# Routed experts of a four-layer transformer: routing weights spread over the rows by DMA from DRAM in place of a picking matmul

## The reference

```python
scores = softmax(xf @ Wg)                        # [4096, 32]
weights, indices = top_k(scores, 4)              # 4 experts for each token
for e in range(32):
    # the first 2048 tokens that chose e, with their weight w
    out = (silu(xg @ W1[e]) * (xg @ W3[e])) @ W2[e] * w[:, None]
    y = y.at[tok].add(out)
z = (silu(xf @ Ws1) * (xf @ Ws3)) @ Ws2
x = x + attention(xn) + y + z
```

## Time and profile before

| | us |
|---|---|
| median of 3 runs | 3521.24 (3521.11 to 3521.61) |
| the profiled execution, its own time | 3524.08 |
| its span in the profile | 3522.1 |
| TensorE busy over the span | 3236.2 (92%) |
| mean granted TensorE clock over the span | 0.96 of full |

### The profile page before, as it was taken

The page is one execution under the profiler, slowest core; times in us unless marked ns, Lnnn a source line. Parts: engine busy times, 40 slices in busy tenths (PEclk is TensorE's granted clock), DMA queues, the critical chain, the costliest instruction groups (busy, mean ns, idle before and its releaser), DMA issues.

```text
span 3522.1 us, 73076 instructions
## 1 busy us (share of the span) xinstructions
PE 3236.2 (92%) x24822; PEld 2369.4 (67%) x24823; DVE 2505.3 (71%) x5419; ACT 2384.3 (68%) x7079; POOL 1901.2 (54%) x1809
## 2 busy tenths in 40 slices
PE   5999969998769996999997999999999999999997
PEld 3777646665558885757665677766777677676775
DVE  6888768883676666444345778887788777877776
ACT  4777748885335555624523888888888888888885
POOL 4222132221235553401203888888888888888884
PEclk9999969999779997999997999999999999999998
DMA  3222132220000003000000000000000000000000
GB/s 104 71 70 73 40 122 73 76 70 1 1 1 1 1 1 103 13 1 1 1 1 13 2 2 2 2 1 2 1 2 1 2 2 2 1 2 2 2 2 25
DMA packets 54894, 78.25 MB, mean 22 GB/s; under 512 B 5952, under 2 KB 43648, under 8 KB 54272
## 3 DMA queue, kind: packets, MB, share of 16 engines
q1 hardware_dynamic: 54528, 73.58, 6.5%
HBM read 54.69 MB, written 18.87 MB: 21 GB/s over the span
## 4 chain that ended last, share of the span: by engine, by line
PE 45%; POOL 6%; ACT 4%; DVE 3%; issue 3%; DVEq 0%; ACTq 0%; POOLq 0%
PE psum L1973 8%; PE psum L1963 7%; PE psum L1988 7%; PE psum L2011 4%; POOL attn_p L2330 4%; PE psum L1460 3%; ACT attn_p L2085 3%; PE psum L1920 2%; POOL attn_qf L2324 2%; PE psum L1385 2%; PE psum L1471 2%; PE psum L1532 2%; PE psum L1551 2%; PE psum L1365 1%; DVE attn_nm L2205 1%
## 5 line engine op out<-in xcount | busy, mean ns | idle before, releaser
L2085 ACT ACTIVATE attn_p<-psum,attn_nm 128x256 f32<-128x256 f32 x1536 | 709.5, 478 | 250.1 <-DVE attn_nm L2205 245.7
L2330 POOL TENSOR_TENSOR attn_p<-attn_p,attn_rinv 128x512 f32<-128x512 f32 x768 | 783.5, 1041 | 133.0 <-DVE attn_rinv L2212 133.0
L2205 DVE TENSOR_REDUCE attn_nm<-psum 128x2 f32<-128x512 f32 x768 | 491.0, 680 | 20.2 <-PE psum L1963 20.0
L1988 PE MATMUL psum<-attn_pt,attn_v 128*64 128x256 f32 x3072 | 416.3, 391 | 32.1 <-DVE attn_ql L2224 27.8
L1973 PEld LDWEIGHTS psum<-sb_kept,attn_p 128*128 128x128 f32 x3072 | 328.3, 140 | 163.4 <-issue 92.3
L1973 PE MATMUL psum<-sb_kept,attn_p 128*128 128x128 f32 x3072 | 427.0, 280 | 7.8 <-POOL attn_p L2330 7.7
L569 ACT ACTIVATE sb_a_p<-psum,sb_a_nm 128x256 f32<-128x256 f32 x1024 | 405.9, 493 | 37.3 <-DVE sb_a_nm L507 34.2
L507 DVE TENSOR_REDUCE sb_a_nm<-psum 128x2 f32<-128x512 f32 x512 | 328.4, 683 | 31.3 <-PE psum L414 19.1
L2085 ACT ACTIVATION_READ_ACCUMULATOR attn_p<-psum,attn_nm 128x1 f32 x1536 | 319.7, 208 | 0.0
L1988 PEld LDWEIGHTS psum<-attn_pt,attn_v 128*64 128x64 f32 x3072 | 192.8, 136 | 180.2 <-issue 57.7
L2218 DVE COPY attn_pt<-psum 128x512 f32<-128x512 f32 x384 | 262.7, 684 | 69.3 <-PE psum L1973 66.7
(11 more groups left out here) (395 smaller groups left out, 7797.3 us busy)
## 6 DMA issues: line engine op xcount, KB each, us to landing
sb_a_spread<-a_spilled SPq DMA_DIRECT2D x128, 256.0 KB, 3.1
a_spilled<-sb_a_part_hi SPq DMA_DIRECT2D x64, 128.0 KB
a_spilled<-sb_a_part_lo SPq DMA_DIRECT2D x64, 128.0 KB
sb_x<-in_L_attn_x SPq DMA_DIRECT2D x4, 512.0 KB, 6.3
sb_wg<-in_L_ffn_Wg SPq DMA_DIRECT2D x1, 2048.0 KB, 11.2
sb_wu<-in_L_ffn_Wu SPq DMA_DIRECT2D x1, 2048.0 KB, 15.9
out<-sb_x SPq DMA_DIRECT2D x4, 512.0 KB, 3.3
sb_table<-in_const SPq DMA_DIRECT2D x1, 1498.0 KB, 7.9
```

Source lines behind the costliest of these rows:

```text
L1988: mm = pe.matmul(O[half(e), :], V[u % 2][:, kt, h * HD3:(h + 1) * HD3], PTs[p % 2][:, e, kt, :], start=(kt == 0), stop=(kt == TB - 1))
L2085: ins = act.activation(Pr[p % 3][:, e, t, :], S(p, e)[:, t * N:(t + 1) * N], ACT.Exp, bias=nm[:, p % 4, e, t:t + 1], accum_out=rsum[:, p % ...
L2205: dve.tensor_reduce(nm[:, p % 4, e, :], S(p, e).rearrange("p (t n) -> p t n", t=TB), AX.X, ALU.max, negate=True).then_inc(maxed.sem, 1)
L2330: pool.tensor_tensor(P3, P3, spread(rinv[:, p % 4, e, :], N), ALU.mult).then_inc(normed.sem, 1)
```

## The change

The picking matmul, its matrix and its operand go. In their place the block's weights are stored to DRAM as 32 rows of 512 (`wrow` to a `routing` box, two boxes in turn), and for each routed unit SP issues a transfer that reads the two rows of the pair, each 64 times, into one of four SBUF buffers `wide` of 128x512. The second multiplication of VectorE then reads `wide` in place of the bank `Wb`. A transfer into a buffer waits for `hid` of the unit four routed units before, which used the buffer last; the block's store must have landed before its first transfer is issued. The constants lose the columns `sel` and `expert` (which was not used). TensorE's `project` waits at p = 0 for the weights of its block to have been moved out of Y.

```diff
@@ ExpertWeights
-        self.picks, self.sel = sb("sel", [P, NP2 * P], F32R), sel
-        self.wp = [sb(f"wp{i}", [P, CH], F32R) for i in range(2)]
...
-        elif i == len(self.parts):
-            act.copy(self.picks[:, :], self.sel).then_inc(self.picked.sem, 1)
...
-        for v in self.wp:
-            pool.memset(v[:, :].bitcast(F32), 0.0).then_inc(self.zeroed.sem, 1)
@@ experts
+        wrow, wide = [sb(f"wrow{i}", [NE2, CH]) for i in range(2)], [sb(f"wide{i}", [P, CH]) for i in range(NW)]
+        boxes = [nc.dram_tensor(f"routing{i}", [NE2, CH], F32, kind="Internal") for i in range(2)]
...
             def move_weights(ch):
                 act.wait_ge(*weight_turned(ch))
-                act.copy(wp[ch % 2][0:NE2, :], Y[ch % 2][0:NE2, :]).then_inc(weight_high.sem, 1)
+                if ch >= 2:
+                    act.wait_ge(*weight_out(16 * (ch - 1) - 1))
+                act.copy(wrow[ch % 2][:, :], Y[ch % 2][0:NE2, :]).then_inc(weight_moved.sem, 1)
...
-            def part_weights(ch):
-                w_ = wp[ch % 2]
-                dve.wait_ge(*weight_high(ch))
-                dve.tensor_tensor(w_[NE2:2 * NE2, :], Y[ch % 2][0:NE2, :], w_[0:NE2, :].bitcast(F32),
-                                  ALU.subtract).then_inc(weight_low.sem, 1)
...
                     if p:
+                        n = ch * NP2 + p - 1
                         c.dve_own(ins)
-                        ins = dve.tensor_tensor(hh[i % 3][:, :], hh[i % 3][:, :], Wb[i % 2][:, :], ALU.mult)
+                        dve.wait_ge(*widened[n % NW](16 * (n // NW + 1) - 1))
+                        ins = dve.tensor_tensor(hh[i % 3][:, :], hh[i % 3][:, :], wide[n % NW][:, :], ALU.mult)
...
-                elif p == 1:
-                    pe.wait_ge(*weight_low(ch))
...
-                if p:
-                    mm = pe.matmul(Wb[i % 2][:, :], picks[:, (p - 1) * P:p * P], wp[b][:, :], start=True, stop=True)
...
-                if p == 0 and ch >= 2:
-                    pe.wait_ge(*added(ch - 2))
+                if p == 0:
+                    pe.wait_ge(*weight_moved(ch))
...
+        def sp_program():
+            for ch in range(NCH):
+                box = boxes[ch % 2]
+                sp.wait_ge(*weight_moved(ch))
+                sp.dma_start(bass.AP(tensor=box, offset=0, ap=[[CH, NE2], [1, CH]]), wrow[ch % 2][:, :]).then_inc(weight_out.sem, 16)
+                sp.wait_ge(*weight_out(16 * (ch + 1) - 1))
+                for p in range(NP2):
+                    n = ch * NP2 + p
+                    if n >= NW:
+                        before = n - NW
+                        sp.wait_ge(*hid(before // NP2 * R + before % NP2 + 1))
+                    src = bass.AP(tensor=box, offset=2 * p * CH, ap=[[CH, 2], [0, HID], [1, CH]])
+                    sp.dma_start(wide[n % NW][:, :], src).then_inc(widened[n % NW].sem, 16)
```

More of the change, by code:

```diff
@@ L63, in const_columns @@
     c["block"] = (p[:, None] // 32) == np.arange(4)[None, :]
[L64 to L69, removed]
     return {k: np.ascontiguousarray(v, dtype=np.float32) for k, v in c.items()}
@@ L1143, with __init__ @@
     R = NP2 + 1
-    def __init__(self, c, sb, w1, w3, w2, ws, sel):
+    def __init__(self, c, sb, w1, w3, w2, ws):
         NP2, R = self.NP2, self.R
@@ L1161, in __init__ @@
         self.high_made, self.low_made = c.steps("moe_high", len(self.parts)), c.steps("moe_low", len(self.parts))
-        self.picked, self.zeroed = c.steps("moe_picked", 1), c.steps("moe_zeroed", 2)
-        self.ends = (self.high_made, self.low_made, self.picked, self.zeroed)
+        self.ends = (self.high_made, self.low_made)
     def act_step(self, i):
@@ L1183, in experts @@
     nc = c.nc
-    pe, act, dve, pool = nc.tensor, nc.scalar, nc.vector, nc.gpsimd
+    pe, act, dve, pool, sp = nc.tensor, nc.scalar, nc.vector, nc.gpsimd, nc.sync
     NP2, R = weights.NP2, weights.R
-    NI = NCH * R
+    NI, NW = NCH * R, 4
     router.cap()
@@ L1191, in experts @@
         hh = [sb(f"h{i}", [P, CH]) for i in range(3)]
-        high, low, picks, wp = weights.high, weights.low, weights.picks, weights.wp
+        high, low = weights.high, weights.low
+        wrow, wide = [sb(f"wrow{i}", [NE2, CH]) for i in range(2)], [sb(f"wide{i}", [P, CH]) for i in range(NW)]
+        boxes = [nc.dram_tensor(f"routing{i}", [NE2, CH], F32, kind="Internal") for i in range(2)]
         down_high, down_low = weights.down_high, weights.down_low
@@ L1196, in experts @@
         out_d = [sb(f"out_d{i}", [P, CH]) for i in range(2)]
-        G, U, Wb, Y = c.banks[0:2], c.banks[2:4], c.banks[4:6], c.banks[6:8]
+        G, U, Y = c.banks[0:2], c.banks[2:4], c.banks[6:8]
         split, split_low = c.steps("split", 1), c.steps("split_low", 1)
-        weight_turned, weight_high, weight_low = (c.steps(f"weight_{k}", NCH) for k in ("turned", "high", "low"))
+        weight_turned, weight_moved, weight_out = (c.steps(f"weight_{k}", n) for k, n in (("turned", NCH), ("moved", NCH), ("out", 16 * NCH)))
+        widened = [c.steps(f"weight_wide{i}", 16 * NCH * NP2 // NW) for i in range(NW)]
         next_cast, next_parted = c.steps("next_cast", NCH - 1), c.steps("next_parted", NCH - 1)
@@ L1253, in dve_program @@
         def dve_program():
-            def part_weights(ch):
-                w_ = wp[ch % 2]
-                dve.wait_ge(*weight_high(ch))
-                dve.tensor_tensor(w_[NE2:2 * NE2, :], Y[ch % 2][0:NE2, :], w_[0:NE2, :].bitcast(F32),
-                                  ALU.subtract).then_inc(weight_low.sem, 1)
-            part_weights(0)
             for i in range(NI + 7):
@@ L1268, in dve_program @@
                     if p:
+                        n = ch * NP2 + p - 1
                         c.dve_own(ins)
-                        ins = dve.tensor_tensor(hh[i % 3][:, :], hh[i % 3][:, :], Wb[i % 2][:, :], ALU.mult)
+                        dve.wait_ge(*widened[n % NW](16 * (n // NW + 1) - 1))
+                        ins = dve.tensor_tensor(hh[i % 3][:, :], hh[i % 3][:, :], wide[n % NW][:, :], ALU.mult)
                     ins.then_inc(hid.sem, 1)
-                    if ch + 1 < NCH and p == 11:
-                        part_weights(ch + 1)
                 if i >= 7 and (i - 7) % R == R - 1:
@@ L1334, in experts @@
         pe_program()
-        c.meet(added, parted, weight_low)
+        sp_program()
+        c.meet(added, parted, weight_moved, *widened)
 E3, SL, F3 = 16, 64, 256
@@ L2413, in program @@
         small_in = c.load("small", *pairs)
-        late = where["sel"][0]
-        table_in = c.load("table", (table[:, 0:late], const[:, 0:late]))
+        table_in = c.load("table", (table[:, :], const))
         mask400, future0, future1 = eb("mask400", [P, P], BF16), eb("fut0", [P, N], BF16), eb("fut1", [P, P], BF16)
@@ L2434, in program @@
                   (w2e[:, :, :], a["L2_ffn_W2"].rearrange("(q e) h d -> (e h) q d", e=2))]
-        pairs.append((table[:, late:width], const[:, late:width]))
         for eng in (pe, act, dve, pool):
@@ L2471, in program @@
         mb = lambda k, s, dt=F32: moe.enter_context(nc.sbuf_tensor(f"moe_{k}", s, dt))
-        expert_weights = ExpertWeights(c, mb, w1e, w3e, w2e, [w2l[f"L2_ffn_Ws{k}"][:, :] for k in (1, 3, 2)], tab("sel"))
+        expert_weights = ExpertWeights(c, mb, w1e, w3e, w2e, [w2l[f"L2_ffn_Ws{k}"][:, :] for k in (1, 3, 2)])
         ffn_ternary(c, "tern", x, xnT, w1[:, :, :], b1, w2[:, :], expert_weights)
```

## The result

The changed kernel takes 3889.7 us (median of 4 runs, 3887.94 to 3892.83) against 3521.4 us (4 runs): a ratio of 1.1042, with a 95% interval of 1.1028 to 1.1057. It is 368 us slower. The forecast was 3929.5 us, 408 us slower, with a range of 3863 to 4021.

The account below looks back on a forecast made before the run. TensorE's ten matmuls a unit bound the kernel; two-engine transfers would replace that bound. Stage: 1.9 + 1.3 + 706.6 + 11.9 + 0.2 + 6.8 = 728.7 us against 320.4, so +408.3 on 3521.24: 3929.5 us, range 3863 to 4021.

Parts of the forecast that it names:

- Two engines: The weights' transfer, with outermost count 2 at its source, was taken to run on two of the 16 DMA engines.
- The length of one, 5.52 us: One 256 KB weights transfer per routed unit: 64 packets of 2 KB on each engine at 86.3 ns.
- The lower bound, 5.00 us: One weights transfer at the rate of the largest packets, 26.2 KB/us for one engine's 131 KB; 3863 us in all.
- Between blocks, 1.7 us: Gap at each of seven block changes: 0.4 us for the store's end plus 1.3 us from issue to first packet.
- The start and the end: Stage edges: first store 1.9 us, 1.3 us to the first packet; 6.8 us from the last weighted multiplication to the end.
- What is hidden: In a unit, everything beside the 5.52 us transfer, matmuls of 2.04 to 3.9 us included; TensorE's clock falls at no cost.
- Queued landings, some 20 us after issue: Sign in the profile after: each weights transfer lands some 20 us after issue, with three queued behind the running one.
- (a): Rival: the weights' transfer gets all 16 engines and TensorE stays the bound; gain 28.9 us, 3492 us; chance 0.05.
- (b): Rival: 16 engines, but VectorE's second multiplication, both inputs in SBUF, and GpSimd's subtraction exclude each other; about 3522 us; chance 0.05.
- 28.9 us: Worth of removing the picking matmul from 128 of 136 units, at 0.226 us each with TensorE full.
- (c): Rival: two engines, and each transfer starts only after the previous landed, 1.5 us more for each of 128; 4121 us; chance 0.03.

Follow-up runs that it names:

- the regrouping: Against two transfers a unit with outermost count 64: U times the weights into a free PSUM bank, then silu(G) times that bank; 3489.3 us, ratio 0.9915.

## Why the prediction was right

**Two engines.** Right, and now shown for the source's side too: shares of 0.13 and 0.25 for counts of 2 and 4 with nothing else changed, and 16 engines by the count of small packets for 64. The step rested on one pair of rows for the destination's side and on the page "DMA: Bandwidth & Descriptors" of the Trainium skill, section "Why a DMA increments its semaphore by 16 and not by 1", for the source's; the runs agree with the page.

**The length of one, 5.52 us.** This is the term that was off. Measured 5.12 us, 80.0 ns for each of 64 packets. In 74 us of the stage (1042 to 1116), where all packets but 42 are of 2 KB (the view of DMA queues: packets, MB, busy share of 16 engines):

```profile
q1 hardware_dynamic: 1918, 3.84, 13.5%
```

0.135 x 16 x 74/1918 = 83 ns of record each, small ones included, and 84 ns in the median for those of 2 KB. Yet in the trace they start 80 ns apart on each of the two engines, so one is still on record when the next begins. The forecast took the length on record for the distance. Its own row corrects it: 391 packets on 16 engines in 2.00 us start at most 81.8 ns apart, where 86.3 ns was put in, and that gives 5.24 us a transfer. The share of 105.5% is this overlap, and not that a packet counts whole where it starts, as the prediction had it. So 0.28 of the 0.40 us come from this reading, and 0.12 remain between 16 busy engines and two. 128 x 0.40 = 51 us of the forecast's 408 are this term. The lower bound, 5.00 us from the largest packets, was the nearer one, but by luck: read by its starts, 0.89 MB in 32 us of engine time, it would have been 4.7.

**Between blocks, 1.7 us.** Measured 7.77 - 5.12 = 2.65 us. Over the seven changes that makes 7 us more. The gap itself was put rightly: at each change no packet starts for 1.63 to 1.79 us (1117.25 to 1118.90 at the first). What the forecast left out is that the store's own packets take their turn on the two engines, and that the new block's first packets are slow: at the first change one took 0.90 us where the others take 0.08.

**The start and the end.** From the move of the weights to the first weighted multiplication 1040.61 - 1031.25 = 9.4 us (forecast 8.9, with a transfer of 5.52 in it), from the last to the end 1719.32 - 1712.42 = 6.9 (forecast 6.8). Together with 671.8 us between the first and the last multiplication they make 688.1, where I had 728.7. The terms of 51 us too much and 7 us too little are most of it; the distances inside a block were not all 5.12 us either, but (671.8 - 7 x 7.77)/120 = 5.15 on the mean, 3 us more. So a part of the error of the packets was made up for by two errors the other way.

**What is hidden.** Right: TensorE's granted clock fell (0.81 on the mean over the stage, between its levels of 2.4 and 1.2 GHz), and at no cost, since each of the 128 multiplications still had to wait for a landing (488.0 us in all, 3.8 a unit, forecast 4.1), and 3.9 us of slow matmuls fit into 5.12. TensorE idled more than a third of the time by the profile's count, not more than half: a matmul of L1276 is on record for 0.49 to 0.54 us there, against 0.39 before.

**Queued landings, some 20 us after issue.** Right for the weights' transfers, if one counts from the beginning of the issue instruction: the sixteenth is issued at 1098.63, and the multiplication that waits for it starts at 1117.51, 18.9 us later; the median of all 128 is 18.8. But the forecast had SP's issue at 0.6 us, and the instruction did not return at once (the landing times below are those of the stores alone, 13.9 us in the median):

```profile
L1325 SPq DMA_DIRECT2D experts_wide<-routing x128: 496/5002/7162, 1033.0 to 1693.8; - x128
L1317 SPq DMA_DIRECT2D routing<-experts_wrow x8: 354/4989/7131, 1031.3 to 1613.9; - x8
...
DMA to landing us min/median/max: 1.6/13.9/15.5
```

The median issue of a `wide` transfer took 5.0 us, about as long as a transfer, where the shortest took 0.5 us. It was no wait for a buffer: for the third and the fourth transfer of the stage all four buffers were still free, and their issues took 3.0 and 5.2 us. When the sixteenth issue returned, at 1103.63, the thirteenth transfer had already been used (1102.47), so two transfers were queued behind the one that ran, and not three. The engines did not run dry inside a block for it, and the time did not change.

**The rivals.** (a) would not have come alone: with 16 engines the kernel became 3536 us, not 3492. (b) was the true second mechanism behind the first; its range of 2.04 to 2.49 us a unit held the 2.38 us, but the middle of 2.27 was 0.11 us too low, and with it the 3522 us. It is also what makes the change, had its transfers been quick, no gain: 32 us to be had from the picks, 46 us given back. Both had to go before 3489 us came out, and then the stage fell by 29.2 us, close to the 28.9 us that 128 matmuls at full pace were worth. (c) fell: on each engine the packets start 80 ns apart from one transfer into the next, but for the small one between them, which leaves no room for a wait.

## What to carry to other kernels

Look at the outermost count of both sides of a DMA before you trust its size: 256 KB took 5.12 us with a 2 there and hid under 2.04 us as two transfers with a 64, for the same bytes. When an operand moves from PSUM to SBUF, check whether the instruction now has two SBUF inputs and whether GpSimd reads SBUF at that time; if so, regroup so that each VectorE instruction keeps one input in PSUM. And a product that picks rows on TensorE is worth replacing only if what replaces it stays under the unit's remaining length on every engine.

## What had not been expected

SP's issue instruction stood for 5.0 us in the median (0.5 us at least) when transfers on two engines were queued, so a long queue also holds up whatever SP would do next. The exclusion lasts for nearly the whole instruction (all but 0.13 us of the multiplication came behind the subtraction), and the blocked one shows as a longer instruction, not as idle time: a 0.69 us multiplication is recorded as 1.67 us in the groups by line, and the busy share of VectorE goes up (190 of 240 us, against 158 after the regrouping) while it does less (200 instructions against 229). Whoever reads busy time alone would take VectorE for slow there.
